# Step inputs of a selective scan replicated by DMA through DRAM instead of by TensorE, and step sizes three pairs deep

## The chip, the cores and the metric

One core of one Trainium2 chip runs the whole program. The metric is the device time of one execution in microseconds, lower is better. The times of a kernel are given as the median of several executions; the profile is one further execution, with its own time.

## The reference, cut to what matters

The program is a chain of four convolution-like layers on an array `x` of shape (16, 32, 128, 128). The change lies in layer 1, in its state-space ("mamba") part. Two directions over a sequence of length 16384, with 18 inner channels and 16 states:

```python
def selective_scan(u, dt, A, Bm, Cm, D):
    dA = jnp.exp(dt[..., None] * A)
    dBu = dt[..., None] * Bm[:, :, None, :] * u[..., None]
    def comb(e1, e2):
        a1, b1 = e1
        a2, b2 = e2
        return (a2 * a1, a2 * b1 + b2)
    _, h = jax.lax.associative_scan(comb, (dA, dBu), axis=1)
    return jnp.einsum('bldn,bln->bld', h, Cm) + u * D

def run(xz_, A_log_):
    xi, z = jnp.split(xz_, 2, axis=-1)
    xi = jax.nn.silu(causal_dwconv1d(xi.transpose(0, 2, 1), conv1d_w, conv1d_b)).transpose(0, 2, 1)
    x_dbl = xi @ x_proj_w.T
    dt = jax.nn.softplus(x_dbl[..., :DT_RANK] @ dt_proj_w.T + dt_proj_b)
    Bm = x_dbl[..., DT_RANK:DT_RANK + D_STATE]
    Cm = x_dbl[..., DT_RANK + D_STATE:]
    y = selective_scan(xi, dt, -jnp.exp(A_log_), Bm, Cm, D_ssm)
    return y * jax.nn.silu(z)
```

So each (batch, channel) row of `dt` and of `dt * u` is needed 16 times, once for each state: for the decay `exp(dt * A)` and for the product with `Bm`.

## The kernel before, in words

The stage is the function `state_space` (from L738). Its work is cut into 128 chunks (`N = 4 * NC`: two directions, two halves of the batch, 32 pieces of 512 positions), which follow one another. A chunk holds 8 batch rows. A tile for the scan has 128 partitions (8 batch rows times 16 states) and 512 columns, and belongs to one of the 18 channels. Two channels make a pair, so a chunk is 9 pairs, p = 0 to 8; channels 0 to 9 are half 0 and channels 10 to 17 are half 1. Each engine runs its own list of instructions in order, and semaphores tie the lists together. The tail of each engine's list for chunk i already holds the projections of chunk i+1.

One pair goes through the engines like this:

- GpSimd (`steps`, L1174) makes the step sizes `dts[:, un, hf, 0]` = softplus and the step inputs `dts[:, un, hf, 1]` = step size times `xi`, 128x512 each, half 0 of the next chunk after its outputs of pair 5 and half 1 after those of pair 7.
- TensorE replicates a channel's 8 rows over the 16 states with a 0/1 matrix `sl`: `rates_of` (L891) into the PSUM tile `pr` (2 banks, one pair deep), and `inputs_of` (L897) into the PSUM tile `pu` (4 banks, two pairs deep). `replicate` (L916) issues the inputs of pair p+1 and the rates of pair p+2. Before both it waits until the scan has left the bank (`wait_inputs`) and until the exponential has read `pr` (`wait_rates`).
- ScalarE (`decays`, L1060) turns `pr` into the decays `da` in SBUF, two pairs ahead; between them it does the gates, the softplus and the copies of the projections of the next chunk, which all go through one PSUM bank `pp` in a fixed order (L1083 to L1109).
- VectorE (`inputs_by_b`, L1131) multiplies `pu` in place with `bs` (L1138, two instructions a pair), and (`scans`, L1140) runs the recurrence (L1148, two a pair): `da` from SBUF, `pu` from PSUM, result `hs` in SBUF, three pairs deep. Twice a chunk `skip` (L1151) adds the direct term to the reduced outputs.
- GpSimd (`outputs`, L1187) carries the last column on (L1193) and multiplies `hs` with `cs` (L1196), both 18 times a chunk, and multiplies with the gate (`gated`, L1180) twice. The scan of pair p+3 waits until the outputs of pair p are done.
- TensorE reduces over the states (`reduce`, L930) and projects out (`out_proj`, L885); ScalarE copies the result to `osb` (L1058), once a chunk and 129 times in all.
- SyncE loads the sequences (L821, six DMAs a chunk) and the rates (L824, L825) of chunk i+2, and stores chunk i-1 (L829).

Of the kernel before, what the change touches and what calls it, by code (L numbers as in the profile page):

```python
# [8 lines left out]
P = 128  # L9
# [728 lines left out]
def state_space(nc, seq, w_x, w_z, conv_rows, conv_b, w_dt, dt_rows, dt_b, w_b, w_c, a_log, keeps, d_skip, w_out,  # L738
# [4 lines left out]
    N = 4 * NC  # L743
    KEEP = D_IN
    USES = 9
    X0, Z0, X1, Z1, DT0, DT1, BB, CC, OUT = range(USES)
    LAST_OF = {0: 1, 1: 1, 2: 3, 3: 3, 4: 4, 5: 6, 6: 6, 7: 8, 8: 8}

    with ExitStack() as ctx:
# [59 lines left out]
        @block.sync  # L809
        def _(sp):  # L810
            weights = ((wx, w_x), (wz, w_z), (crow, conv_rows), (wdt, w_dt), (drow, dt_rows), (wb, w_b), (wc, w_c), (wo, w_out), (sl, sel), (slt, sel_t))
            for dst, src in weights:
                sp.dma_start(dst[:], src).then_inc(w_load, 16)
            for n, src in enumerate((conv_b, dt_b, d_skip)):
                sp.dma_start(cols[:, n, :], src).then_inc(w_load, 16)

            def load(i, u):
                taps = (0, 1, 1, 2, 2, 3)
                rows = seq[at(i)].rearrange("i p n -> (i p) n")
                for tap, (tile, to, first, n) in zip(taps, TAP_PARTS):  # L820
                    sp.dma_start(sq[to:to + n, u, tile, :], rows[first:first + n, tap:tap + LC]).then_inc(s_in[u], 16)  # L821

            def load_rates(i, u):
                sp.dma_start(al[:, u, 0:D_IN], a_log[at(i)].rearrange("i p n -> (i p) n")).then_inc(a_in[u], 16)  # L824
                sp.dma_start(al[:, u, KEEP:], keeps[at(i), :].broadcast_to([NB, 1])).then_inc(a_in[u], 16)  # L825

            def store(i, u, use):
                sp.wait_ge(pp_drained, use + 1)
                sp.dma_start(mixed[at(i)].rearrange("i p n -> (i p) n"), osb[:, u, :]).then_inc(stored[u], 16)  # L829

            for n in range(2):
                load(n, n)
                load_rates(n, n)

            def chunk(i, j, u, last):

                sp.wait_ge(pp_drained, use_of(i, Z1) + 1)
                load(i + 2, u)
                sp.wait_ge(carry_ready, i * D_IN + D_IN)
                load_rates(i + 2, u)  # L840
                store(i, u, use_of(i + 1, OUT))

            with sp.Fori(0, N // 2 - 1) as j:
                for u in range(2):
                    chunk(j * 2 + u, j, u, False)
            store(N - 2, 0, use_of(N - 1, OUT))
            store(N - 1, 1, use_of(N, 0))
            store(N, 0, use_of(N, 1))
            sp.wait_ge(stored[0], 16 * (N // 2 + 2))
            sp.wait_ge(stored[1], 16 * (N // 2 + 1))  # L850

        @block.tensor
        def _(pe):
# [37 lines left out]
            def rates_of(i, u, p, part):  # L891
                hf, q, run = place(2 * p + part)
                rows = slice(32 * q, 32 * q + 32)
                pe.matmul(pr[:, LC * part:LC * (part + 1)], sl[rows, run, :], dts[rows, u, hf, 0, :],  # L894
                          start=True, stop=True, tile_position=(32 * q, 0)).then_inc(rates_done, 1)

            def inputs_of(i, u, p, part):  # L897
                hf, q, run = place(2 * p + part)
                rows = slice(32 * q, 32 * q + 32)
                bank = 2 * ((u + p) % 2) + part  # L900
                pe.matmul(pu[:, LC * bank:LC * (bank + 1)], sl[rows, run, :], dts[rows, u, hf, 1, :],  # L901
                          start=True, stop=True, tile_position=(32 * q, 0)).then_inc(inputs_done, 1)

            def wait_inputs(i, p):

                if p in (0, HALF_PAIRS):
                    pe.wait_ge(dtu_ready, i * 2 + (1 + p // HALF_PAIRS))
                pe.wait_ge(scan_done, i * D_IN + (2 * p + 4))

            def wait_rates(i, p):  # L910

                if p in (0, HALF_PAIRS):
                    pe.wait_ge(dt_ready, i * 2 + (1 + p // HALF_PAIRS))
                pe.wait_ge(exp_done, i * D_IN + (2 * p + 2))

            def replicate(i, u, p, last):  # L916

                ahead = [(i, u, p + k) if p + k < PAIRS else (i + 1, 1 - u, p + k - PAIRS) for k in (1, 2)]
                if not (last and p + 1 >= PAIRS):
                    wait_inputs(ahead[0][0], ahead[0][2])  # L920
                if not (last and p + 2 >= PAIRS):
                    wait_rates(ahead[1][0], ahead[1][2])
                for part in range(2):
                    if not (last and p + 1 >= PAIRS):
                        inputs_of(*ahead[0], part)
                for part in range(2):
                    if not (last and p + 2 >= PAIRS):
                        rates_of(*ahead[1], part)
# [33 lines left out]
            wait_inputs(0, 0)
            wait_rates(0, 0)
            for part in range(2):
                inputs_of(0, 0, 0, part)
            for part in range(2):
                rates_of(0, 0, 0, part)
            wait_rates(0, 1)
            for part in range(2):
                rates_of(0, 0, 1, part)  # L970
# [40 lines left out]
        def _(act):  # L1011
# [103 lines left out]
        def _(dve):  # L1115
# [15 lines left out]
            def inputs_by_b(i, u, p):  # L1131
# [1773 lines left out]
```

## Time and profile before

| | |
|---|---|
| median of 3 executions | 20994.22 us (20714.11, 21013.87, 20994.22) |
| profiled execution | 20821.64 us, of which its span is 20820.1 us |
| state-space stage in the profile | starts near 7180 us, ends near 12760 us |
| busy share of the span | PE 79%, DVE 67%, ACT 62%, POOL 46% |
| mean granted TensorE clock | 0.855 of 2.4 GHz |

PE is TensorE, DVE VectorE, ACT ScalarE, POOL GpSimd, SP SyncE. A tile is named with the prefix of its stage: `l1m` is the state-space stage, `l1y` the one after it, `l1d` the one after that, `l3a` a late one. "Idle before" an instruction is time in which its engine did nothing, with what ended it behind the arrow.

### The profile page before, as it was taken

How to read it: one execution, taken by the hardware profiler on the slowest of the kernel's cores; microseconds unless marked ns; L12 is line 12 of the kernel's file. 1: busy time of each engine (PE TensorE's matmuls, PEld its weight loads, DVE VectorE, ACT ScalarE, POOL GpSimd, SP SyncE). 2: the span in 40 equal slices, each digit the busy share in tenths (PEclk: the TensorE clock that was granted, in tenths of full speed). 3: DMA queues.
4: the chain of work that ended last, by engine and by line, in shares of the span. 5: the costliest groups of instructions: out<-in, count | busy, mean ns of one | idle time of the engine just before them, and what ended most of it. 6: DMA issues, size and time to landing. Idle time of an engine off the chain costs nothing. (4 is left out here: it accounts for less than half of the span.)

```text
span 20820.1 us, 421401 instructions
## 1 busy us (share of the span) xinstructions
PE 16358.0 (79%) x158640; PEld 6982.2 (34%) x158640; DVE 14027.1 (67%) x13848; ACT 12953.3 (62%) x21322; POOL 9553.7 (46%) x7800
## 2 busy tenths in 40 slices
PE   6888888888845388888888887699989996336997
PEld 2333333333311022222222222355454453004664
DVE  8999999999951377777777775465565566123322
ACT  6899999988943277777777774466666665220101
POOL 5787877877720177777777775011111111000002
PEclk9999999999977688888888888677787788667988
DMA  2000000000049400000000003221112112993333
GB/s 74 12 11 12 11 12 11 12 12 11 12 114 163 113 17 17 17 17 17 17 17 17 17 17 74 32 31 28 31 31 31 29 31 77 186 209 81 79 68 124
DMA packets 1433366, 986.00 MB, mean 47 GB/s; under 512 B 783816, under 2 KB 1296944, under 8 KB 1399864
## 3 DMA queue, kind: packets, MB, share of 16 engines
q1 hardware_dynamic: 1335848, 837.05, 19.7%
q0 software_dynamic: 17408, 67.11, 1.2%
q10 hardware_dynamic: 79056, 66.70, 1.0%
q8 instruction: 793, 12.99, 0.3%
q14 instruction: 261, 2.14, 0.0%
HBM read 759.05 MB, written 211.63 MB: 47 GB/s over the span
## 5 line engine op out<-in xcount | busy, mean ns | idle before, releaser
L270 DVE TENSOR_TENSOR l_mx<-l_p_v,l_puN 128x2048 f32<-128x2048 f32 x2560 | 5635.7, 2281 | 142.4 <-PE l_p_s L485 129.6
L485 PE MATMUL l_p_s<-l_mx,l_w2z 128*32 128x512 f32 x32768 | 3818.9, 610 | 582.5 <-ACT l_mx L397 313.0
L290 POOL TENSOR_TENSOR l_mx<-l_pv,l_puP 128x2048 f32<-128x2048 f32 x1024 | 3715.6, 3645 | 317.9 <-PE l_p_s L485 312.1
L1196 POOL TENSOR_TENSOR l1m_hc<-l1m_hs,l1m_cs 128x512 f32<-128x512 f32 x2304 | 2922.8, 1269 | 8.5 <-DVE l1m_hs L1148 8.1
L1148 DVE TENSOR_TENSOR_SCAN l1m_hs<-l1m_da,l1m_carry,l1m_pu 128x512 f32<-128x512 f32 x2304 | 2824.1, 1268 | 106.1 <-ACT l1m_da L1066 2.2
L1790 ACT ACTIVATE l1d_ab<-l1d_pt 128x1024 f32<-128x1024 f32 x2304 | 2311.9, 1024 | 611.5 <-DVE l1d_hat L1668 305.6
L416 ACT ACTIVATE l_mx<-l_pv,l_puP 128x128 f32<-128x128 f32 x8192 | 2446.8, 393 | 0.8
L1668 DVE TENSOR_SCALAR l1d_hat<-l1d_ab 128x1024 f32<-128x1024 f32 x2304 | 1923.2, 836 | 443.8 <-ACT l1d_ab L1790 321.0
L1138 DVE TENSOR_TENSOR l1m_pu<-l1m_pu,l1m_bs 128x512 f32<-128x512 f32 x2304 | 1477.1, 687 | 1100.9 <-PE l1m_pu L901 1100.9
L1587 PE MATMUL l1d_po<-l1d_hat,l1d_ring 128*32 128x128 f32 x36864 | 1799.7, 322 | 358.7 <-DVE l1d_hat L1668 233.2
L485 PEld LDWEIGHTS l_p_s<-l_mx,l_w2z 128*32 128x32 f32 x32768 | 982.3, 112 | 3017.5 <-issue 1764.6
L397 ACT ACTIVATE l_mx<-l_mx 128x2048 f32<-128x2048 f32 x1024 | 1954.4, 1909 | 50.8 <-POOL l_mx L290 50.4
L1841 POOL TENSOR_TENSOR l1d_res<-l1d_res,l1d_so 128x2048 f32<-128x2048 f32 x32 | 119.4, 3731 | 3951.8 <-DVE l1d_to L1727 3949.5
L1066 ACT ACTIVATE l1m_da<-l1m_pr,l1m_an 128x512 f32<-128x512 f32 x2304 | 1458.9, 684 | 565.3 <-PE l1m_pr L894 399.9
L901 PE MATMUL l1m_pu<-l1m_dts,l1m_sl 32*128 32x512 f32 x4608 | 1416.0, 691 | 480.4 <-ACT l1m_da L1066 470.7
L1569 PE MATMUL l1d_pg<-l1d_wz,l1d_im 32*128 32x288 f32 x5120 | 1472.5, 656 | 22.1 <-DMA l1d_im<-x_after 10.1
L1655 DVE COPY l1d_ring<-l1d_pg 128x288 f32<-128x288 f32 x1280 | 585.7, 458 | 1323.5 <-PE l1d_pg L1569 1321.8
L1587 PEld LDWEIGHTS l1d_po<-l1d_hat,l1d_ring 128*32 128x32 f32 x36864 | 1030.3, 124 | 1262.9 <-issue 807.2
L894 PE MATMUL l1m_pr<-l1m_dts,l1m_sl 32*128 32x512 f32 x4608 | 1403.2, 687 | 2.7 <-ACT l1m_da L1066 2.7
L2064 POOL TENSOR_TENSOR l3a_lm<-l3a_lmask,l3a_ln 128x1320 f32<-128x1320 f32 x16 | 47.8, 2990 | 2381.2 <-ACT l3a_ln L2015 2381.2
L1776 ACT ACTIVATE l1d_ring<-l1d_pg 128x288 f32<-128x288 f32 x1280 | 526.3, 411 | 877.5 <-PE l1d_pg L1569 876.8
L1552 PE MATMUL l1d_pt<-l1d_yt,l1d_rw 32*128 32x512 bf16 x4608 | 1047.5, 450 | 18.8 <-issue 17.2
(330 smaller groups left out, 22896.5 us busy)
## 6 DMA issues: line engine op xcount, KB each, us to landing
n_xt<-x_after SPq DMA_DIRECT2D x48, 2048.0 KB
l1o_img<-x_after SPq DMA_DIRECT2D x32, 2032.0 KB, 17.2
l_img<-x_after SPq DMA_DIRECT2D x32, 2032.0 KB, 16.9
l1m_sq<-seq SPq DMA_DIRECT2D x256, 144.0 KB
n_xt<-in_x_dram SPq DMA_DIRECT2D x16, 2048.0 KB
l_xs<-in_x_dram SPq DMA_DIRECT2D x128, 256.0 KB, 2.9
x_after<-l_ot SPq DMA_DIRECT2D x128, 256.0 KB, 2.4
l1o_img<-x_after SPq DMA_DIRECT2D x16, 2048.0 KB, 16.9
```

The source lines that it names most:

```text
L270: v.tensor_tensor(mx[:, r % QB, :, :, :], columns.unsqueeze(1).broadcast_to([P, 4, G, P]), rows.broadcast_to([P, 4, G, P]), ALU.max).then_ ...
L290: g.tensor_tensor(mx[:, r % QB, :, :, :], pv[:, u, :, :].unsqueeze(1).broadcast_to([P, 4, G, P]), rows.broadcast_to([P, 4, G, P]), ALU.add ...
L397: act.activation(tile, tile, ACT.Relu).then_inc(max_by_g, 1)
L416: ins = act.activation(mx[:, r % QB, q, t, :], pv[:, u, t, :], ACT.Relu, bias=puP[:, u, t, R * q + r:R * q + r + 1])
L485: ins = pe.matmul(p_s[R * q:R * (q + 1), 512 * u:512 * (u + 1)], w2z[:, 31 - r:63 - r], mx[:, r % QB, q, :, :].rearrange("p t v -> p (t v) ...
L1138: dve.tensor_tensor(tile, tile, bs[:, u, :], ALU.mult).then_inc(dbu_done, 1)
L1148: dve.tensor_tensor_scan(hs[:, p % 3, part, :], da[:, p % 3, part, :], pu[:, LC * bank:LC * (bank + 1)], carry[:, u, c:c + 1], ALU.mult, A ...
L1196: g.tensor_tensor(hc[:, (3 * u + p) % 6, part, :], hs[:, p % 3, part, :], cs[:, u, :], ALU.mult).then_inc(hc_done, 1)
L1569: pe.matmul(pg[:, 512 * half_strip:512 * half_strip + KO], im[C * g:C * (g + 1), :, col_at(g, j)], wz[C * g:C * (g + 1), u, :], start=True ...
L1587: ins = pe.matmul(po[C * g:C * (g + 1), 512 * (s % 2):512 * (s % 2) + P], ring[:, (8 * u + s + k) % RING, g, k, :], hat[:, m % 3, n % 2, P ...
L1668: v.tensor_scalar(hat[:, m % 3], ab[:, m % 2], 1.0, 1.0, ALU.min, ALU.subtract).then_inc(hat_done, 1)
L1790: act.activation(ab[:, m % 2].rearrange("p a n -> p (a n)"), pt[:, 1024 * (m % 2):1024 * (m % 2 + 1)], ACT.Abs).then_inc(abs_done, 1)
```

## The change

- The step inputs are no longer replicated by TensorE. SyncE writes a half of them (128x512, 256 KB) to a DRAM tensor `steps_u`, waits until the write has landed (`write_steps`), and then reads each channel's 8 rows back with 16 copies of each row, into one of six SBUF slots of `rp` (`replicas`, two DMAs of 256 KB a pair).
- The product with `bs` is one VectorE instruction over a pair, 128x1024, in place in `rp`, and the scan reads `rp`. Both tensor inputs of the product, and both of the scan, now lie in SBUF.
- `pu` is gone; `pr` has 6 banks, three pairs deep. `replicate` issues the rates of pair p+3 alone and waits only for the exponential of pair p and for new step sizes.
- SyncE's list is written out for all 128 chunks. In it, the replicas of pair p+6 follow the scan of pair p; the write of half 0 of the next chunk stands at p = 3 and that of half 1 at p = 8; the load of the sequences stands at p = 2, the loads of the rates and the store at the chunk's end.

```diff
+    SLOTS = 6
+    steps_u = nc.dram_tensor("step_inputs", [2, 2, P, LC], F32).ap()
...
+        rp = m.sb("rp", [NB, SLOTS, 2, LC])
...
-        pr = m.bank("pr", 2)
-        pu = m.bank("pu", 4)
+        pr = m.bank("pr", 6)
...
+            def write_steps(n, un, hf):
+                sp.wait_ge(dtu_ready, n * 2 + (hf + 1))
+                sp.dma_start(steps_u[un, hf], dts[:, un, hf, 1, :]).then_inc(steps_out, 16)
+                sp.wait_ge(steps_out, n * 32 + (16 * hf + 16))
+            def replicas(un, p):
+                slot = (3 * un + p) % SLOTS
+                for part in range(2):
+                    hf, q, run = place(2 * p + part)
+                    first = 32 * q + HB * run
+                    sp.dma_start(rp[:, slot, part, :], steps_u[un, hf, first:first + HB].unsqueeze(1).broadcast_to([HB, D_STATE, LC])
+                                 ).then_inc(rep_in[slot], 16)
...
+            def chunk(i, u, more, last):
+                for p in range(PAIRS):
+                    q = p + SLOTS
+                    if q < PAIRS or not last:
+                        sp.wait_ge(scan_done, i * D_IN + (2 * p + 8))
+                    if q < PAIRS:
+                        replicas(u, q)
+                    elif not last:
+                        if q - PAIRS in (0, HALF_PAIRS):
+                            write_steps(i + 1, 1 - u, (q - PAIRS) // HALF_PAIRS)
+                        replicas(1 - u, q - PAIRS)
+                    if p == 2 and more:
+                        sp.wait_ge(pp_drained, use_of(i, Z1) + 1)
+                        load(i + 2, u)
+                if more:
+                    sp.wait_ge(carry_ready, i * D_IN + D_IN)
+                    load_rates(i + 2, u)
+                store(i, u, use_of(N, 0) if last else use_of(i + 1, OUT))
...
             def replicate(i, u, p, last):
...
+                n, un, q = (i, u, p + 3) if p + 3 < PAIRS else (i + 1, 1 - u, p + 3 - PAIRS)
+                if not (last and p + 3 >= PAIRS):
+                    if q in (0, HALF_PAIRS):
+                        pe.wait_ge(dt_ready, n * 2 + (1 + q // HALF_PAIRS))
+                    pe.wait_ge(exp_done, i * D_IN + (2 * p + 4))
+                    for part in range(2):
+                        rates_of(n, un, q, part)
...
-                dve.wait_ge(inputs_done, i * D_IN + (2 * p + 2))
-                for part in range(2):
-                    bank = 2 * ((u + p) % 2) + part
-                    tile = pu[:, LC * bank:LC * (bank + 1)]
-                    dve.tensor_tensor(tile, tile, bs[:, u, :], ALU.mult).then_inc(dbu_done, 1)
+                slot, uses = (3 * u + p) % SLOTS, (PAIRS * u + p) // SLOTS
+                dve.wait_ge(rep_in[slot], j * (32 * 3) + 32 * (uses + 1))
+                tile = rp[:, slot]
+                dve.tensor_tensor(tile, tile, bs[:, u, :].unsqueeze(1).broadcast_to([NB, 2, LC]), ALU.mult).then_inc(dbu_done, 2)
...
-                    dve.tensor_tensor_scan(hs[:, p % 3, part, :], da[:, p % 3, part, :], pu[:, LC * bank:LC * (bank + 1)],
+                    dve.tensor_tensor_scan(hs[:, p % 3, part, :], da[:, p % 3, part, :], rp[:, (3 * u + p) % SLOTS, part, :],
                                            carry[:, u, c:c + 1], ALU.mult, ALU.add).then_inc(scan_done, 1)
```

## Rows read from the trace of the kernel before

**Rows 1.** All instructions of L1058, the last copy of each chunk: min/median/max, first and last start.

```profile
L1058 ACT ACTIVATE l1m_osb<-l1m_pp x129: 593/593/595, 7235.6 to 12759.1; 72x512 f32<-72x512 f32 x129
```

**Rows 2.** Busy time by engine in 500 us of the stage (clock, DMA share, GB/s last).

```profile
10000.00:10500.00 500.00, 434.40 (x1670) 132.49 (x1668) 395.21 (x439) 351.90 (x471) 371.58 (x483) 0.87 0.06 16
```

**Rows 3.** The page's groups by line: busy us, mean ns | idle before, releaser.

```profile
L1138 DVE TENSOR_TENSOR l1m_pu<-l1m_pu,l1m_bs 128x512 f32<-128x512 f32 x2304 | 1477.1, 687 | 1100.9 <-PE l1m_pu L901 1100.9
...
L901 PE MATMUL l1m_pu<-l1m_dts,l1m_sl 32*128 32x512 f32 x4608 | 1416.0, 691 | 480.4 <-ACT l1m_da L1066 470.7
```

**Rows 4.** VectorE in order of time in one chunk: start us, us, instructions, idle before.

```profile
10041.67 1.30 DVE L1138 TENSOR_TENSOR l1m_pu<-l1m_pu,l1m_bs 128x512 f32<-128x512 f32 x2 [6.03 <-PE l1m_pu L901]
...
10056.75 1.30 DVE L1138 TENSOR_TENSOR l1m_pu<-l1m_pu,l1m_bs 128x512 f32<-128x512 f32 x2 [2.51 <-PE l1m_pu L901]
...
10060.50 1.27 DVE L1138 TENSOR_TENSOR l1m_pu<-l1m_pu,l1m_bs 128x512 f32<-128x512 f32 x2
10061.87 2.45 DVE L1148 TENSOR_TENSOR_SCAN l1m_hs<-l1m_da,l1m_carry,l1m_pu 128x512 f32<-128x512 f32 x2
```

**Rows 5.** ScalarE's waits in the 500 us of rows 2: us in total, times, longest.

```profile
ACT l1m_da L1066 <- PE l1m_pr L894: 35.0, 43, 1.4
...
ACT l1m_da L1066 <- DVE l1m_hs L1148: 15.3, 12, 1.3
```

**Rows 6.** Products from SBUF alone, before the stage's chunks start: durations ns min/median/max.

```profile
L1126 DVE TENSOR_TENSOR l1m_wtap<-l1m_wx,l1m_crow x1: 949/949/949, 7143.4 to 7143.4; 96x768 f32<-96x768 f32 x1
...
L1128 DVE TENSOR_TENSOR l1m_wdtm<-l1m_wdt,l1m_drow x2: 411/412/414, 7144.2 to 7144.6; 128x256 f32<-128x256 f32 x2
```

**Rows 7.** VectorE lines with one tensor input in PSUM: durations ns min/median/max.

```profile
L1138 DVE TENSOR_TENSOR l1m_pu<-l1m_pu,l1m_bs x2304: 671/690/700, 7181.8 to 12746.5; 128x512 f32<-128x512 f32 x192
...
L1148 DVE TENSOR_TENSOR_SCAN l1m_hs<-l1m_da,l1m_carry,l1m_pu x2304: 1252/1268/1282, 7185.3 to 12748.5; 128x512 f32<-128x512 f32 x192
...
L1352 DVE TENSOR_TENSOR l1y_v<-l1y_acc,l1y_base x16: 2277/2286/2287, 12801.3 to 13045.2; 72x2048 f32<-72x2048 f32 x16
```

**Rows 8.** VectorE lines with all operands in SBUF: durations ns min/median/max.

```profile
L1668 DVE TENSOR_SCALAR l1d_hat<-l1d_ab x2304: 668/685/5830, 13216.1 to 17561.4; 128x1024 f32<-128x1024 f32 x192
...
L1361 DVE TENSOR_SCALAR l1y_y<-l1y_v x16: 1223/1224/4973, 12804.9 to 13058.0; 72x2048 f32<-72x2048 f32 x16
...
L2118 DVE TENSOR_SCALAR l3a_lns<-l3a_ln,l3a_st x16: 3129/3194/3249, 18840.3 to 20024.9; 128x264 f32<-128x264 f32 x16
```

**Rows 9.** VectorE and GpSimd in order of time, two places of the later stages.

```profile
12836.55 1.22 DVE L1356 TENSOR_SCALAR l1y_v<-l1y_v 72x2048 f32<-72x2048 f32 x1
12837.81 4.97 DVE L1361 TENSOR_SCALAR l1y_y<-l1y_v 72x2048 f32<-72x2048 f32 x1
...
12836.94 4.76 POOL L1280 TENSOR_TENSOR l1y_r<-l1y_y,l1y_piece 72x2048 f32<-72x2048 f32 x1 [3.82 <-ACT l1y_piece L1302]
12843.78 4.07 POOL L1285 TENSOR_TENSOR l1y_r<-l1y_r,l1y_piece 72x2048 f32<-72x2048 f32 x1 [2.08 <-issue]
...
13547.95 4.80 DVE L1668 TENSOR_SCALAR l1d_hat<-l1d_ab 128x1024 f32<-128x1024 f32 x1
...
13547.35 4.86 POOL L1850 TENSOR_TENSOR l1d_res<-l1d_res,l1d_xr 128x2048 f32<-128x2048 f32 x1
```

**Rows 10.** GpSimd's groups in the 500 us of rows 2: busy us, mean ns | idle before.

```profile
L1196 POOL TENSOR_TENSOR l1m_hc<-l1m_hs,l1m_cs 128x512 f32<-128x512 f32 x206 | 261.4, 1269 | 0.0
L1193 POOL TENSOR_TENSOR l1m_carry<-l1m_hs,l1m_al 128x1 f32<-128x1 f32 x207 | 39.2, 189 | 113.7 <-DVE l1m_hs L1148 112.3
L1178 POOL TENSOR_TENSOR l1m_dts<-l1m_dts,l1m_xi 128x512 f32<-128x512 f32 x24 | 30.4, 1267 | 1.9
```

**Rows 11.** SyncE's issues: six in order of time; then two DMA groups, KB each, us to landing.

```profile
10066.94 2.81 SPq L821 DMA_DIRECT2D l1m_sq<-seq  x6
...
l_xs<-in_x_dram SPq DMA_DIRECT2D x128, 256.0 KB, 2.9
x_after<-l_ot SPq DMA_DIRECT2D x128, 256.0 KB, 2.4
```

More of the change, by code:

```diff
@@ L784, in state_space @@
         py = m.bank("py")
-        pr = m.bank("pr", 2)
-        pu = m.bank("pu", 4)
+        pr = m.bank("pr", 6)
         (w_load, w_ready, a_exp, a_ready, pp_full, pp_drained, ab, e3, lg_ready, dt_ready, dtu_ready,
-         rates_done, inputs_done, exp_done, dbu_done, scan_done, carry_ready, hc_done, y_done, y1_done, y2_done) = (m.sem(n) for n in (
+         rates_done, exp_done, dbu_done, scan_done, carry_ready, hc_done, y_done, y1_done, y2_done) = (m.sem(n) for n in (
              "w_load w_ready a_exp a_ready pp_full pp_drained ab e3 lg_ready dt_ready dtu_ready "
-             "rates_done inputs_done exp_done dbu_done scan_done carry_ready hc_done y_done y1_done y2_done").split())
+             "rates_done exp_done dbu_done scan_done carry_ready hc_done y_done y1_done y2_done").split())
         s_in = [m.sem("s_in0"), m.sem("s_in1")]
         a_in = [m.sem("a_in0"), m.sem("a_in1")]
+        steps_out = m.sem("steps_out")
+        rep_in = [m.sem(f"rep_in{n}") for n in range(SLOTS)]
         stored = [m.sem("stored0"), m.sem("stored1")]
@@ L833, in _ @@
                 load_rates(n, n)
[L835 to L847, printed above, removed]
+            for hf in range(2):
+                write_steps(0, 0, hf)
+            for p in range(SLOTS):
+                replicas(0, p)
+            def chunk(i, u, more, last):
[16 more added lines that the diff above has]
+                store(i, u, use_of(N, 0) if last else use_of(i + 1, OUT))
+            for i in range(N):
+                chunk(i, i % 2, i < N - 2, i == N - 1)
             store(N, 0, use_of(N, 1))
@@ L893, in rates_of @@
                 rows = slice(32 * q, 32 * q + 32)
-                pe.matmul(pr[:, LC * part:LC * (part + 1)], sl[rows, run, :], dts[rows, u, hf, 0, :],
+                bank = 2 * (p % 3) + part
+                pe.matmul(pr[:, LC * bank:LC * (bank + 1)], sl[rows, run, :], dts[rows, u, hf, 0, :],
                           start=True, stop=True, tile_position=(32 * q, 0)).then_inc(rates_done, 1)
-            def inputs_of(i, u, p, part):
-                hf, q, run = place(2 * p + part)
-                rows = slice(32 * q, 32 * q + 32)
-                bank = 2 * ((u + p) % 2) + part
[L901 to L914, printed above, removed]
-            def replicate(i, u, p, last):
[L918 to L922, printed above, removed]
-                for part in range(2):
[L924 to L928, printed above, removed]
+            def replicate(i, u, p, last):
+                n, un, q = (i, u, p + 3) if p + 3 < PAIRS else (i + 1, 1 - u, p + 3 - PAIRS)
[5 more added lines that the diff above has]
+                        rates_of(n, un, q, part)
             def reduce(i, u, pairs):
@@ L961, in _ @@
             c_proj(0, 0, 2)
[L962 to L970, printed above, removed]
+            pe.wait_ge(dt_ready, 1)
+            for p in range(3):
+                for part in range(2):
+                    rates_of(0, 0, p, part)
             def chunk(i, j, u, last):
@@ L1065, in decays @@
                 for part in range(2):
-                    act.activation(da[:, p % 3, part, :], pr[:, LC * part:LC * (part + 1)], ACT.Exp,
+                    act.activation(da[:, p % 3, part, :], pr[:, LC * (2 * (p % 3) + part):LC * (2 * (p % 3) + part + 1)], ACT.Exp,
                                    scale=an[:, u, 2 * p + part:2 * p + part + 1]).then_inc(exp_done, 1)
@@ L1129, in _, with inputs_by_b @@
             ins.then_inc(w_ready, 1)
-            def inputs_by_b(i, u, p):
+            def inputs_by_b(i, j, u, p):
                 if p == 0:
                     dve.wait_ge(pp_drained, use_of(i, BB) + 1)
-                dve.wait_ge(inputs_done, i * D_IN + (2 * p + 2))
-                for part in range(2):
-                    bank = 2 * ((u + p) % 2) + part
-                    tile = pu[:, LC * bank:LC * (bank + 1)]
-                    dve.tensor_tensor(tile, tile, bs[:, u, :], ALU.mult).then_inc(dbu_done, 1)
+                slot, uses = (3 * u + p) % SLOTS, (PAIRS * u + p) // SLOTS
+                dve.wait_ge(rep_in[slot], j * (32 * 3) + 32 * (uses + 1))
+                tile = rp[:, slot]
+                dve.tensor_tensor(tile, tile, bs[:, u, :].unsqueeze(1).broadcast_to([NB, 2, LC]), ALU.mult).then_inc(dbu_done, 2)
             def scans(i, u, p):
@@ L1145, in scans @@
                 for part in range(2):
-                    bank = 2 * ((u + p) % 2) + part
                     c = 2 * p + part
-                    dve.tensor_tensor_scan(hs[:, p % 3, part, :], da[:, p % 3, part, :], pu[:, LC * bank:LC * (bank + 1)],
+                    dve.tensor_tensor_scan(hs[:, p % 3, part, :], da[:, p % 3, part, :], rp[:, (3 * u + p) % SLOTS, part, :],
                                            carry[:, u, c:c + 1], ALU.mult, ALU.add).then_inc(scan_done, 1)
@@ L1159, in chunk @@
                 for p in range(PAIRS):
-                    inputs_by_b(i, u, p)
+                    inputs_by_b(i, j, u, p)
                     scans(i, u, p)
```

## The prediction

> **What bounds the kernel now.** I read the stage first: the last copy of a chunk (L1058) runs 129 times [rows 1], so a chunk takes (12759.1 - 7235.6) / 128 = 43.15 us, and every microsecond a chunk is worth 128 us. The busy times of 500 us inside the stage [rows 2], times 43.15 / 500, give each engine's work a chunk: PE 37.5, DVE 34.1, ACT 30.4, POOL 32.1 us. None is full. Then the groups by line: DVE waits 1100.9 us in the stage for the replicated inputs in `pu`, 8.6 us a chunk [rows 3]. 34.1 + 8.6 = 42.7 of 43.15: DVE's work and this one wait make the chunk. DVE in order of time shows where: 6.03 us at one pair, 2.51 at another, and in between a pair is 1.27 us of products and 2.45 us of scans with nothing before them [rows 4]. TensorE's list is in order, and the inputs of the next pair stand behind projections that wait for ScalarE; that is why they come late.
>
> **Parts that take work away.** The inputs leave TensorE: 1416.0 us, 11.1 us a chunk [rows 3]. TensorE at 26.4 us then bounds nothing, even if its granted clock fell from 0.87 to the lower of its two levels, 0.5 or 1.2 GHz (26.4 x 0.87 / 0.5 = 46 us, under the chunk that I forecast). DVE's wait for `pu` goes. The product becomes one instruction of 1024 columns with both inputs in SBUF: 768 columns take 949 ns and 256 take 412 [rows 6], 1.05 ns a column, so 1.22 us in place of 1.27 [rows 4], 0.5 us a chunk less. The scan keeps its 2.45 us a pair, since its pace (1268 ns for 512 columns [rows 7], against 690 for a product) is that of the recurrence. DVE's work becomes 33.6 us.
>
> **DMAs and waits that it adds, at nothing.** SyncE issues 20 more DMAs a chunk. Six in a row take 2.81 us [rows 11], 0.47 each, so 9.4 us of a queue that is else nearly empty. Their traffic: 16 GB/s over 500 us is 8.0 MB, and a share of 0.06 of 16 engines is 480 engine-us [rows 2], 60 us a MB, so 15.7 engine-us for 256 KB. 20 of them are 315, or 19.7 us a chunk on all 16 engines and 39.3 if half of the engines take part. Both fit under the chunk that I forecast.
> How many engines a DMA uses no row shows. The Trainium skill ("DMA: Bandwidth & Descriptors", section on why a DMA increments its semaphore by 16) says that it is the largest number up to 16 that divides the slowest dimension on both sides; here these are 8 and 128, so 8 engines and the 39.3.
> SyncE waits in `write_steps` for the next chunk's step inputs. Queued behind it are replicas of the next chunk alone, the rates and the store, none due before the chunk's end; the replicas of pairs 6 to 8 stand ahead. Half 0 is made after GpSimd's pair 5. GpSimd can lag by three pairs (`hs`), so at worst the scans are then at pair 8, and one pair is left for two POOL instructions (2.5 us), a write and a read (2.4 and 2.9 us [rows 11]) and issues. That can be some 3 us late. While DVE waits for it, GpSimd works off its arrears, which DVE would meet later; I take nothing, and 6 us a chunk (the write, the read and the issues in full) as the upper end. TensorE's wait for new step sizes moves one pair ahead (p = 6 and p = 2); behind it stand `c_proj` and a reduction, due at the next chunk's first outputs. I take nothing; uncovered it costs no more than the scans of the pair by which it moved, 2.45 us, and the 6 us cover that.
>
> **What decides: two SBUF inputs beside GpSimd.** So far each product and scan read one tensor from PSUM. Such lines never vary beside GpSimd: 671 to 700, 1252 to 1282, 2277 to 2287 ns [rows 7]. Lines whose operands all lie in SBUF do: 668 to 5830 ns, 1223 to 4973, and 264 columns that always take 3.1 us or more [rows 8]. Order of time shows why [rows 9]. DVE's L1361 starts 0.87 us after POOL's 4.76 us instruction and ends at 12842.78, 1.08 us after it: it did its 1.22 us of work when POOL was done. L1668 the same, 0.54 us after a POOL instruction of 4.86. And POOL's L1280, begun under DVE's L1356, takes 4.76 where L1285 of the same shape takes 4.07: it waited until L1356 ended. The two exclude each other for a whole instruction, and about 0.14 us (1.22 - 1.08) is saved at each handover.
> After the change every product and scan has both tensor inputs in SBUF, and GpSimd works 32.1 us a chunk on SBUF. Rows 8 are single-input lines at two columns a ns or nearly; a two-input line at one column a ns beside GpSimd no row shows. The bounds: no exclusion (as rows 7, which have the operations), or full exclusion (as rows 8, which have the place of the operands). I take full exclusion: what parts the varying lines from the steady ones in this trace is where the operands lie; L1352 is a two-input product of 2048 columns and is steady with one of them in PSUM.
> The Trainium skill ("SBUF — State Buffer", section "Who interferes with whom") says that a VectorE instruction with two SBUF inputs contends with a GpSimd instruction that reads SBUF, the second to start being blocked until the first is done. That is the case which no row shows; by it the sum is the one below, without it that of the first rival.
>
> **The sum.** A chunk is then DVE's work and POOL's end to end.
> - Lower end, each instruction less 0.14: DVE 9 x (1.08 + 2 x 1.13) = 30.1; POOL 24 of 128x512 (18 outputs, 2 gates, 4 steps, all like 1267 ns [rows 10]) x 1.13 = 27.1; 18 carries of 0.19 [rows 10] less 0.14 = 0.9. Together 58.1 us.
> - Upper end, nothing saved: 9 x (1.22 + 2.45) = 33.0, and POOL's 32.1: 65.1 us.
> `skip`, with one input in PSUM, lies beside POOL. I take the middle, 61.6 us, 18.45 more than now: x 128 = 2362 us on the profiled execution's 20821.6, so 23180 us. The median shown lies 0.8% above the profiled execution; I leave that to the range.
>
> **The rivals.**
> 1. No exclusion at this pace (ends on the other side). DVE needs 33.6 us and ScalarE's chain is next: 30.4 us of work, and of its idle 148.1 us in rows 2 the waits for the rates (35.0) and for the scan (15.3) [rows 5] go, which leaves 97.8, 8.4 us a chunk. 38.8 us a chunk: 4.35 x 128 = 557 less, 20265 us, 2.7% faster; 33.6 us would be 19600. For it: the products and scans of rows 7 never varied. Against: they had PSUM inputs. It decides if the scan's mean stays at 1.27 us beside POOL.
> 2. Only the product excludes, the scan does not (it takes a column every 2.5 ns). Each of 9 products waits for one POOL instruction, 1.13: DVE 33.6 + 10.2 = 43.8 us, 0.65 x 128 = 83 more, 20905 us.
> 3. The replicas bound: on 4 engines, or at twice the time a packet on 8, 78.6 us a chunk, 35.4 x 128 = 4530 more, 25350 us. For it: 16 copies of one row come from one place in DRAM. Against: the stage moves 16 GB/s now [rows 2], so there is room, and the slots are six pairs deep.
>
> **How the numbers follow.** 0.80 for the forecast: all of rows 8 vary and none of rows 7, but none has this pace with two inputs. 0.12 for the first rival, 0.05 for the second, 0.03 for the third. The forecast's own ends are 58.1 us (20821.6 + 14.95 x 128 = 22735) and 65.1 + 6 = 71.1 us (24400); 1.5% below for the spread of the runs shown gives 22400 to 24400, which holds the 0.80. A measurement of this kernel tells about 2% from no change. Slower by over 2%: the forecast and the third rival, 0.83. Within 2%: the second, and a quarter of the first, 0.08. Faster: the rest of the first, 0.09.
>
> **What would show it.** Right: the scan's durations spread far above 1.27 us, GpSimd's outputs above 1.27 us, and DVE and POOL are each stretched so that their busy times overlap on paper although a chunk is near 61 us; ScalarE waits for the scan (`da` free) where it waited for rates; DVE hardly waits for a DMA into `rp`. Wrong: scans and outputs steady at 1.27 us, a chunk under 43 us (first rival); only the product stretched (second); DVE idle before the product until a DMA lands, in every pair (third). If it is in the first pair of a chunk alone, the late write of half 0 was under-priced.

## The result and the profile after

The kernel after takes 23104.89 us (median of 4, 23035.26 to 23158.41), the one before beside it 20955.86 us: 1.1048 times as long, with a 95% interval of 1.0968 to 1.1128 (the quotient of the two medians is 1.1026). The forecast was 23180 us. The profiled execution of after took 23076.47 us, with a span of 23074.9 and a mean granted clock of 0.799.

The last copy of a chunk again gives the chunk's time, as [rows 1] did (durations min/median/max, first and last start):

```profile
L1062 ACT ACTIVATE l1m_osb<-l1m_pp x129: 593/593/598, 7255.0 to 14816.2; 72x512 f32<-72x512 f32 x129
```

(14816.2 - 7255.0) / 128 = 59.07 us a chunk for 43.15, so 2038 of the 2255 us by which the span grew lie in the stage. Nearly all the rest, 199 us, lies in the stage `l1d`, whose code is unchanged: 4544.8 us from its first to its last matmul for 4346.0, at a granted clock of 0.73 where the profile of before has 0.79 (each the mean of a stretch with both levels in it). Its most frequent matmul, before and then after:

```profile
L1587 PE MATMUL l1d_po<-l1d_hat,l1d_ring x36864: 269/273/423, 13216.9 to 17562.6; 128*32 128x128 f32 x200
L1589 PE MATMUL l1d_po<-l1d_hat,l1d_ring x36864: 269/297/423, 15276.2 to 19820.7; 128*32 128x128 f32 x200
```

The same 500 us as in [rows 2], then the page's groups by line, for [rows 3, 7, 10]:

```profile
10000.00:10500.00 500.00, 366.24 (x887) 104.11 (x884) 430.63 (x243) 251.51 (x339) 442.59 (x350) 0.72 0.30 102
```

```profile
L1150 DVE TENSOR_TENSOR_SCAN l1m_hs<-l1m_da,l1m_carry,l1m_rp 128x512 f32<-128x512 f32 x2304 | 4822.5, 2132 | 698.2 <-POOL l1m_carry L1195 575.1
...
L1198 POOL TENSOR_TENSOR l1m_hc<-l1m_hs,l1m_cs 128x512 f32<-128x512 f32 x2304 | 3467.7, 1505 | 3.5 <-DVE l1m_hs L1150 3.5
...
L1195 POOL TENSOR_TENSOR l1m_carry<-l1m_hs,l1m_al 128x1 f32<-128x1 f32 x2286 | 2007.4, 878 | 733.1 <-DMA l1m_al<-in_keeps_dram 721.1
...
L1141 DVE TENSOR_TENSOR l1m_rp<-l1m_rp,l1m_bs 128x1024 f32<-128x1024 f32 x1152 | 1730.3, 1502 | 273.2 <-DMA l1m_rp<-step_inputs 273.2
```

DVE and POOL look nearly full, 86% and 89% of the window, although their work hardly changed. The mean durations say why: a scan takes 2132 ns where it took 1268, an output 1505 for 1269, and a carry, which works on one column, 878 for 189. That is time spent waiting inside an instruction, and it counts as busy. Two true waits are new: POOL's 721.1 us for a DMA into `al`, the rates, 5.6 us a chunk, and DVE's 575.1 us for POOL's carry behind it. The wait for the replicas is 273.2 us. Its longest, 44.3 us, is at the start of the stage; the rest is 1.8 us a chunk, and falls on the chunk's first pair.

VectorE and GpSimd in order of time, within one chunk (start us, us, idle before in brackets):

```profile
10083.18 4.53 DVE L1150 TENSOR_TENSOR_SCAN l1m_hs<-l1m_da,l1m_carry,l1m_rp 128x512 f32<-128x512 f32 x2 [1.33 <-POOL l1m_carry L1195]
10087.63 1.19 DVE L1141 TENSOR_TENSOR l1m_rp<-l1m_rp,l1m_bs 128x1024 f32<-128x1024 f32 x1
10088.91 4.43 DVE L1150 TENSOR_TENSOR_SCAN l1m_hs<-l1m_da,l1m_carry,l1m_rp 128x512 f32<-128x512 f32 x2
```

```profile
10083.08 1.26 POOL L1198 TENSOR_TENSOR l1m_hc<-l1m_hs,l1m_cs 128x512 f32<-128x512 f32 x1
10084.30 1.10 POOL L1195 TENSOR_TENSOR l1m_carry<-l1m_hs,l1m_al 128x1 f32<-128x1 f32 x1
10085.36 1.27 POOL L1198 TENSOR_TENSOR l1m_hc<-l1m_hs,l1m_cs 128x512 f32<-128x512 f32 x1
10086.59 1.10 POOL L1195 TENSOR_TENSOR l1m_carry<-l1m_hs,l1m_al 128x1 f32<-128x1 f32 x1
10087.65 2.33 POOL L1198 TENSOR_TENSOR l1m_hc<-l1m_hs,l1m_cs 128x512 f32<-128x512 f32 x1
```

The first scan of the pair waits for the output that ends at 10084.34. The carry that POOL issues next waits for the scan, and so takes 1.10 us. Then comes an output, under which the second scan waits, and so on: one scan and one output every 2.29 us. The output at 10087.65 begins with the product at 10087.63, and ends 1.16 us after it.

SyncE in order of time, then its waits for the writes in the window (us in total, times, longest):

```profile
10039.78 0.34 SPq L838 DMA_DIRECT2D step_inputs<-l1m_dts  x1
10041.78 6.34 SPq L847 DMA_DIRECT2D l1m_rp<-step_inputs  x10
10052.41 0.34 SPq L838 DMA_DIRECT2D step_inputs<-l1m_dts  x1
10060.68 1.21 SPq L847 DMA_DIRECT2D l1m_rp<-step_inputs  x2
10061.93 0.46 SPq L828 DMA_DIRECT2D l1m_al<-in_a_log_dram  x1
10062.43 0.43 SPq L829 DMA_DIRECT2D l1m_al<-in_keeps_dram  x1
```

```profile
SPq L847 <- DMA step_inputs<-l1m_dts: 64.4, 16, 9.0
```

The write of half 0 is followed 2.0 us later by the first replica that needs it. The write of half 1 is issued behind ten replicas of 256 KB on the same queue, and its successor comes only 8.3 us later; until then the DMA engines stay half busy (a share of 0.48 to 0.69 from 10048 to 10060 us, 0.02 in the two us after). Over the stage this second write takes 3.3 to 10.2 us, with a median of 5.9. The rates stand behind that; `al` lands when GpSimd has waited 7.70 us for it.

### The profile page after: what moved, and what is told of

It is laid out like the page before. It is cut to its first block and busy times, and to the rows that moved or that the text cites. A ratio compares the mean times of both kernels' runs of the same rounds, so it can differ in the third digit from the quotient of the medians.

```text
span 23074.9 us, 411139 instructions
## 1 busy us (share of the span) xinstructions
PE 17335.3 (75%) x154032; PEld 7173.7 (31%) x154032; DVE 16273.5 (71%) x12696; ACT 12919.8 (56%) x21322; POOL 12288.8 (53%) x7800
## 3 DMA queue, kind: packets, MB, share of 16 engines
q14 instruction: 291, 2.38, 0.0%
## 5 line engine op out<-in xcount | busy, mean ns | idle before, releaser
L1150 DVE TENSOR_TENSOR_SCAN l1m_hs<-l1m_da,l1m_carry,l1m_rp 128x512 f32<-128x512 f32 x2304 | 4822.5, 2132 | 698.2 <-POOL l1m_carry L1195 575.1
L1198 POOL TENSOR_TENSOR l1m_hc<-l1m_hs,l1m_cs 128x512 f32<-128x512 f32 x2304 | 3467.7, 1505 | 3.5 <-DVE l1m_hs L1150 3.5
L1195 POOL TENSOR_TENSOR l1m_carry<-l1m_hs,l1m_al 128x1 f32<-128x1 f32 x2286 | 2007.4, 878 | 733.1 <-DMA l1m_al<-in_keeps_dram 721.1
L1589 PE MATMUL l1d_po<-l1d_hat,l1d_ring 128*32 128x128 f32 x36864 | 1900.9, 337 | 334.1 <-DVE l1d_hat L1670 216.0
L926 PE MATMUL l1m_pr<-l1m_dts,l1m_sl 32*128 32x512 f32 x4608 | 1688.1, 818 | 430.5 <-POOL l1m_dts L1178 425.0
L1141 DVE TENSOR_TENSOR l1m_rp<-l1m_rp,l1m_bs 128x1024 f32<-128x1024 f32 x1152 | 1730.3, 1502 | 273.2 <-DMA l1m_rp<-step_inputs 273.2
L1571 PE MATMUL l1d_pg<-l1d_wz,l1d_im 32*128 32x288 f32 x5120 | 1539.0, 685 | 21.1 <-DMA l1d_im<-x_after 9.7
L1589 PEld LDWEIGHTS l1d_po<-l1d_hat,l1d_ring 128*32 128x32 f32 x36864 | 1080.2, 129 | 1317.1 <-issue 876.8
L901 PE MATMUL l1m_pp<-l1m_xi,l1m_wdtm 128*128 128x512 f32 x1024 | 800.1, 926 | 689.2 <-ACT l1m_sz L1034 673.9
L1554 PE MATMUL l1d_pt<-l1d_yt,l1d_rw 32*128 32x512 bf16 x4608 | 1101.8, 473 | 24.1 <-issue 22.6
```

What stands on the lines that cost most here:

```text
L1141: dve.tensor_tensor(tile, tile, bs[:, u, :].unsqueeze(1).broadcast_to([NB, 2, LC]), ALU.mult).then_inc(dbu_done, 2)
L1195: g.tensor_tensor(carry[:, 1 - u, c:c + 1], hs[:, p % 3, part, LC - 1:], al[:, 1 - u, KEEP:], ALU.mult).then_inc(carry_ready, 1)
L1198: g.tensor_tensor(hc[:, (3 * u + p) % 6, part, :], hs[:, p % 3, part, :], cs[:, u, :], ALU.mult).then_inc(hc_done, 1)
L1589: ins = pe.matmul(po[C * g:C * (g + 1), 512 * (s % 2):512 * (s % 2) + P], ring[:, (8 * u + s + k) % RING, g, k, :], hat[:, m % 3, n % 2, P ...
```

## The experiments

The theory is that of the forecast: a VectorE instruction with two SBUF inputs and a GpSimd instruction exclude each other, so that the one that starts second waits until the first is done. Its rivals are the new DMAs and waits, and an effect of the product alone. "Before" beside the first four was 20941.94 us (median of 7), beside the last three 20935.15 (median of 17). Ratios are to it, with 95% intervals; they differ by up to 0.3% from the quotients of the medians shown. The time of a chunk is read from one profiled execution of each kernel.

**The scan alone, in the kernel before.** No DMA of the change; the product goes to SBUF (VectorE reads one input from PSUM there) and the scan reads two inputs from SBUF.

```diff
+        di = m.sb("di", [NB, 4, LC])
-                    dve.tensor_tensor(tile, tile, bs[:, u, :], ALU.mult).then_inc(dbu_done, 1)
+                    dve.tensor_tensor(di[:, bank, :], tile, bs[:, u, :], ALU.mult).then_inc(dbu_done, 1)
-                    dve.tensor_tensor_scan(hs[:, p % 3, part, :], da[:, p % 3, part, :], pu[:, LC * bank:LC * (bank + 1)],
+                    dve.tensor_tensor_scan(hs[:, p % 3, part, :], da[:, p % 3, part, :], di[:, bank, :],
```

> The kernel before, with one edit: the product is written to an SBUF tile, and the scan reads that in place of PSUM. So the scan has two SBUF inputs, the product one; there is no DMA path and no new order. Exclusion whenever both tensor inputs of a VectorE instruction lie in SBUF: the scan's mean rises from 1.27 to about 2 us, GpSimd's outputs and carries rise too, and a chunk is at least the 18 scans less the handover (18 x 1.13 = 20.3 us) and GpSimd's 28 to 32 us, 48 to 53 us in place of 43.15, so 21450 to 22100 us. Rival, the time of the changed kernel comes from its DMA path and its new waits: scan steady at 1.27 us, chunk within 1 us of 43.15, time unchanged. Rival, only the product excludes: the same as the second.

Measured: 21654.7 us (4 executions), 1.0348 [1.0292, 1.0403]; 49.13 us a chunk. Groups of 500 us of this kernel:

```profile
L1149 DVE TENSOR_TENSOR_SCAN l1m_hs<-l1m_da,l1m_carry,l1m_di 128x512 f32<-128x512 f32 x184 | 367.6, 2036 | 8.3
L1139 DVE TENSOR_TENSOR l1m_di<-l1m_pu,l1m_bs 128x512 f32<-128x512 f32 x182 | 115.0, 670 | 6.5 <-PE l1m_pu L902 6.4
...
L1197 POOL TENSOR_TENSOR l1m_hc<-l1m_hs,l1m_cs 128x512 f32<-128x512 f32 x182 | 230.3, 1265 | 0.0
L1194 POOL TENSOR_TENSOR l1m_carry<-l1m_hs,l1m_al 128x1 f32<-128x1 f32 x182 | 125.9, 692 | 35.3 <-DVE l1m_hs L1149 35.3
```

Moving one operand of the scan from PSUM to SBUF stretches it to 2036 ns, while the product with one PSUM input stays at 670. GpSimd's carries rise to 692 ns as expected; its outputs, expected to rise too, stay at 1265: here it is the scan and the carry that do the waiting. The exclusion does not need the change's DMAs, and it holds for a scan, at one column every 2.5 ns, which the second rival denied.

**The product alone, in the kernel after.** The product writes to PSUM and the scan reads from there. The product's own inputs both stay in SBUF. `pr` gives up a pair of its banks for it.

```diff
+        pu = m.bank("pu", 2)
-                dve.tensor_tensor(tile, tile, bs[:, u, :].unsqueeze(1).broadcast_to([NB, 2, LC]), ALU.mult).then_inc(dbu_done, 2)
+                dve.wait_ge(scan_done, i * D_IN + (2 * p + 6))
+                dve.tensor_tensor(pu[:].rearrange("p (b n) -> p b n", b=2), tile, bs[:, u, :].unsqueeze(1).broadcast_to([NB, 2, LC]), ALU.mult).then_inc(dbu_done, 2)
```

> The changed kernel, with the product written to two PSUM banks and the scan reading it there, so that only the product has two SBUF inputs; the rates are two pairs deep in four banks. Exclusion by operands: the scan is steady at 1.27 us, the product's mean lies between 1.2 and 2.4 us, and a chunk is VectorE's 33.6 us and at most 9 waits of 1.13, so 40 to 46 us, 20400 to 21200 us. Rival, the DMA path and the waits: these are all still there, so near the changed kernel's 59 us a chunk. Rival, only the product excludes: also near 59.

Measured: 22107.75 us (4), 1.0588 [1.0521, 1.0655]; 51.43 us a chunk, far above what was expected. The page's groups of this kernel:

```profile
L1152 DVE TENSOR_TENSOR_SCAN l1m_hs<-l1m_da,l1m_carry,l1m_pu 128x512 f32<-128x512 f32 x2304 | 2823.5, 1267 | 1202.3 <-POOL l1m_carry L1197 849.7
L1143 DVE TENSOR_TENSOR l1m_pu<-l1m_rp,l1m_bs 128x1024 f32<-128x1024 f32 x1152 | 1905.7, 1654 | 302.7 <-DMA l1m_rp<-step_inputs 193.1
...
L1197 POOL TENSOR_TENSOR l1m_carry<-l1m_hs,l1m_al 128x1 f32<-128x1 f32 x2286 | 844.6, 369 | 1477.2 <-DMA l1m_al<-in_keeps_dram 1463.4
```

The scan is steady at 1267 ns and the product is stretched (mean 1654), as forecast, but POOL now waits 1463.4 us for `al`, 11.4 us a chunk. The late rates, seen as a symptom in the kernel after, look like a cost of their own, which the next three experiments test.

**No VectorE instruction with two SBUF inputs.** As the last one, with `bs` in PSUM too; everything else of the change stays (`pr` one pair deep makes room).

```diff
-        bs = m.sb("bs", [NB, 2, LC])
-        pr = m.bank("pr", 6)
+        pr = m.bank("pr", 2)
+        pu = m.bank("pu", 2)
+        bs = m.bank("bs", 2)
-                dve.tensor_tensor(tile, tile, bs[:, u, :].unsqueeze(1).broadcast_to([NB, 2, LC]), ALU.mult).then_inc(dbu_done, 2)
+                dve.tensor_tensor(pu[:].rearrange("p (b n) -> p b n", b=2), tile, bs[:, LC * u:LC * (u + 1)].unsqueeze(1).broadcast_to([NB, 2, LC]), ALU.mult).then_inc(dbu_done, 2)
```

> The changed kernel, with the copy of B in two PSUM banks and the product written to two PSUM banks, so that product and scan each have one SBUF input; the rates go back to one pair deep, two pairs ahead. The replicas by DMA, the write through DRAM and SyncE's order are as in the changed kernel. Exclusion: product near 1.2 us and scan at 1.27 us, both steady, GpSimd's outputs steady at 1.27 us, and a chunk is ScalarE's chain, 38.8 to 43 us, so 20250 to 20900 us. Rival, the DMA path and the new waits are the cost: near 59 us a chunk, 23000 us.

Measured: 21866.92 us (4), 1.0445 [1.0376, 1.0514]; 50.05 us a chunk. Groups of the same 500 us:

```profile
L1153 DVE TENSOR_TENSOR_SCAN l1m_hs<-l1m_da,l1m_carry,l1m_pu 128x512 f32<-128x512 f32 x180 | 220.6, 1267 | 109.4 <-POOL l1m_carry L1198 79.2 <-ACT l1m_da L1072 25.2 <-POOL l1m_hc L1201 1.0
L1144 DVE TENSOR_TENSOR l1m_pu<-l1m_rp,l1m_bs 128x1024 f32<-128x1024 f32 x90 | 110.5, 1228 | 20.6 <-DMA l1m_rp<-step_inputs 14.0
...
L1201 POOL TENSOR_TENSOR l1m_hc<-l1m_hs,l1m_cs 128x512 f32<-128x512 f32 x180 | 228.3, 1269 | 0.0
L1198 POOL TENSOR_TENSOR l1m_carry<-l1m_hs,l1m_al 128x1 f32<-128x1 f32 x179 | 34.2, 191 | 125.5 <-DMA l1m_al<-in_keeps_dram 125.5
```

Every duration is back at its free value, carry included. The exclusion is gone, and 9.0 us a chunk went with it. The expected 43 us or less was not reached, because POOL now waits 125.5 us in 500 for the rates, and DVE 79.2 us for POOL.

**The rates earlier.** The kernel after with the loads of the rates at p = 2, ahead of both writes.

```diff
-                if more:
-                    sp.wait_ge(carry_ready, i * D_IN + D_IN)
-                    load_rates(i + 2, u)
+                        sp.wait_ge(carry_ready, i * D_IN + D_IN)
+                        load_rates(i + 2, u)
```

> The changed kernel, with the loads of the rates moved from the chunk's end to p = 2, ahead of the writes of the step inputs that SyncE waits for. GpSimd's 721 us of waits for that load go. If VectorE and GpSimd together are the bound, VectorE used that time for its own instructions, and a chunk stays between 58 and 59 us: 0 to 150 us less. Rival, the wait is on the path: 5.6 us a chunk, some 720 us less, 22400 us.

Measured: 22816.02 us (4), 1.0916 [1.0848, 1.0983]; 57.02 us a chunk. Groups of 500 us:

```profile
L1149 DVE TENSOR_TENSOR_SCAN l1m_hs<-l1m_da,l1m_carry,l1m_rp 128x512 f32<-128x512 f32 x158 | 350.8, 2258 | 6.6
...
L1197 POOL TENSOR_TENSOR l1m_hc<-l1m_hs,l1m_cs 128x512 f32<-128x512 f32 x157 | 228.0, 1452 | 0.0
L1194 POOL TENSOR_TENSOR l1m_carry<-l1m_hs,l1m_al 128x1 f32<-128x1 f32 x158 | 174.8, 1106 | 0.0
```

POOL waits for nothing any more and yet the chunk is only 2.05 us shorter, more than the 1 us expected at most and far less than the rival's 5.6: while POOL stood and waited in the kernel after, DVE ran free (at 10061.26 a pair of scans took 2.46 us there, for the 4.53 shown), so the wait of 5.6 us was in good part used. This is the exclusion nearly by itself: a chunk is DVE's and POOL's work end to end, 57.02 us where the sum's lower end was 58.1.

**Both undone together.** The edits of the last two experiments in one kernel.

```diff
-        pr = m.bank("pr", 6)
+        pr = m.bank("pr", 2)
+        pu = m.bank("pu", 2)
+        bs = m.bank("bs", 2)
...
+                        sp.wait_ge(carry_ready, i * D_IN + D_IN)
+                        load_rates(i + 2, u)
```

> The kernel of the earlier run in which product and scan have one PSUM input each, and besides the loads of the rates at p = 2, as in the run that moved them alone. In that earlier run the exclusion was gone and a chunk still took 50.05 us, with GpSimd waiting 13.9 us a chunk for the rates. Two costs, exclusion and late rates, each hiding the other: a chunk falls to ScalarE's chain, 38.8 to 43 us, 20250 to 20950 us, and the replicas and the write through DRAM cost next to nothing. Rival, a third cost sits in the DMA path (8 engines for a replica, 39 us a chunk by the estimate): VectorE waits for the replicas in every pair, and a chunk stays at 45 to 50 us.

Measured: 20771.47 us (10), 0.9942 [0.9906, 0.9978]; 41.09 us a chunk, within what was expected. Its window, and VectorE's groups in it:

```profile
10000.00:10500.00 500.00, 434.35 (x1311) 129.25 (x1309) 418.62 (x354) 374.36 (x503) 393.26 (x513) 0.90 0.42 147
```

```profile
L1152 DVE TENSOR_TENSOR_SCAN l1m_hs<-l1m_da,l1m_carry,l1m_pu 128x512 f32<-128x512 f32 x220 | 269.6, 1267 | 40.1 <-ACT l1m_da L1071 32.5 <-DVE l1m_pu L1143 1.2
L1143 DVE TENSOR_TENSOR l1m_pu<-l1m_rp,l1m_bs 128x1024 f32<-128x1024 f32 x110 | 135.1, 1228 | 23.0 <-DMA l1m_rp<-step_inputs 14.9 <-DVE l1m_hs L1152 0.2
L1159 DVE SCALAR_TENSOR_TENSOR l1m_y<-l1m_xi,l1m_cols,l1m_py 128x512 f32<-128x512 f32 x24 | 17.6, 735 | 17.8 <-PE l1m_py L948 17.8
```

The two causes account for the loss: 41.09 + 9.0 for the late rates (50.05), or + 15.9 for the exclusion (57.02), and together 59.07, since each hides part of the other (`pr` is one pair deep in the first two of these, three pairs in the others). The replicas are not a third: their traffic is higher here (a DMA share of 0.42 and 147 GB/s) at 41.09 us a chunk, and the wait for them is 14.9 us in 500. What the change would have brought without the two causes is 2.06 us a chunk, or 0.6% of the whole time, against the 10% that it cost. DVE's 8.6 us for `pu` gave way to waits for the decays (32.5 us in 500), the reduced outputs (17.8) and the replicas (14.9).

**Outputs that only write.** The kernel after with early rates, and GpSimd's 18 outputs made by a memset: the product with C is left out, and so is its reading of SBUF. The carry keeps reading; the wait for a free output slot now stands ahead of it.

```diff
-                g.tensor_tensor(hc[:, (3 * u + p) % 6, part, :], hs[:, p % 3, part, :], cs[:, u, :], ALU.mult).then_inc(hc_done, 1)
+                g.memset(hc[:, (3 * u + p) % 6, part, :], 0.5).then_inc(hc_done, 1)
```

> The changed kernel with the rates loaded at p = 2, and GpSimd's 18 outputs a chunk made by writing a constant to SBUF, without reading; this leaves out the product with C. Product and scan keep their two SBUF inputs. GpSimd's carries, gates and steps still read. If VectorE waits only for GpSimd instructions that read SBUF: the scan's mean falls from 2.26 us to under 1.7, the writes overlap the scans, and a chunk is 39 to 46 us. Rival, any GpSimd instruction on SBUF excludes: each of 18 writes still takes its turn, the scan's mean stays at 1.9 us or more, and a chunk is 9 x 3.3 us of VectorE and GpSimd's turns end to end, 48 us or more.

Measured: 20929.91 us (one execution), 43.31 us a chunk. The scan's group in 500 us, then VectorE and GpSimd in order of time:

```profile
L1149 DVE TENSOR_TENSOR_SCAN l1m_hs<-l1m_da,l1m_carry,l1m_rp 128x512 f32<-128x512 f32 x204 | 272.7, 1377 | 23.3 <-ACT l1m_da L1069 15.8
```

```profile
10061.51 2.24 DVE L1140 TENSOR_TENSOR l1m_rp<-l1m_rp,l1m_bs 128x1024 f32<-128x1024 f32 x1 [3.68 <-DMA l1m_rp<-step_inputs]
...
10066.17 1.20 DVE L1140 TENSOR_TENSOR l1m_rp<-l1m_rp,l1m_bs 128x1024 f32<-128x1024 f32 x1
```

```profile
10061.40 1.27 POOL L1183 TENSOR_TENSOR l1m_y<-l1m_y,l1m_sz 128x512 f32<-128x512 f32 x1
...
10066.17 0.52 POOL L1197 MEMSET l1m_hc<- 128x512 f32 x1
10066.65 0.76 POOL L1196 TENSOR_TENSOR l1m_carry<-l1m_hs,l1m_al 128x1 f32<-128x1 f32 x1
```

The scan's mean falls from 2258 to 1377 ns, as expected if only reads exclude. Beside a memset begun at the same time, the product takes its 1.20 us and the memset 0.52, so that it has ended 0.68 us before the product; beside the gate, which reads, it takes 2.24. The carry behind the memset, which reads one column, waits for the product's end. So it is GpSimd's reading that excludes, however little it reads. The memset is also shorter than an output, so the chunk's time alone would not separate the two; the durations do.

**The order on TensorE, in the kernel before.** The change's aim, inputs that come in time, without leaving PSUM: the inputs of pair p+1 are issued before the wait for the rates' bank, and the projection for the gate one pair later.

```diff
-                if not (last and p + 2 >= PAIRS):
-                    wait_rates(ahead[1][0], ahead[1][2])
                 for part in range(2):
...
                         inputs_of(*ahead[0], part)
+                if not (last and p + 2 >= PAIRS):
+                    wait_rates(ahead[1][0], ahead[1][2])
...
-                        z_proj(n, un, 1)
...
                         if p == 3:
+                            z_proj(n, un, 1)
                             dt_proj(n, un, 0)
```

> The kernel before with TensorE's list reordered and nothing else: the inputs of pair p+1 are issued before the wait for the rates' bank, and the second z projection of the next chunk goes behind the replication at p = 3. If VectorE's 8.6 us a chunk for the replicated inputs came from TensorE's order: most of that wait goes, and a chunk is 39 to 41.5 us, 20250 to 20650 us, faster than both kernels. Rival, the wait only moves to the decays, since ScalarE's chain is as late as TensorE's inputs: the scan waits for ScalarE and a chunk stays within 1 us of 43.15.

Measured: 20664.54 us (6), 0.9889 [0.9843, 0.9934]; 40.77 us a chunk. DVE's wait in the kernel before, then DVE's group in this one, each in the same 500 us, show the part of the wait that is left:

```profile
DVE l1m_pu L1138 <- PE l1m_pu L901: 95.5, 32, 6.0
...
L1138 DVE TENSOR_TENSOR l1m_pu<-l1m_pu,l1m_bs 128x512 f32<-128x512 f32 x220 | 141.4, 689 | 67.9 <-PE l1m_pu L901 67.9
```

67.9 us in 500 is 5.5 us a chunk, for 8.2 in the same window of before: a third of the wait has gone, not most of it as expected. The granted clock in this window also rose, from 0.87 to 0.94, and no run tells how much of the gain is the clock's. The chunk lies in the range expected, the time 15 us above its range. This version has the lowest median of the study, though its interval overlaps with that of "Both undone together", and it changes only the order.

## Why the prediction was right, and where its steps were off

- **What bounds the kernel before: borne out in part.** Issuing the inputs earlier shortened the chunk by 2.38 us, 2.7 of the wait having gone, with a higher granted clock. The other 5.5 us of the wait were not removed.
- **Full exclusion: shown from both sides.** It appears with one operand moved to SBUF, and goes when the operands return to PSUM. The rule of the Trainium skill ("SBUF — State Buffer", section "Who interferes with whom") says that two SBUF inputs contend with a GpSimd instruction that reads SBUF and not with one that only writes; the products of 2.24 and 1.20 us above agree with both halves. One reading behind the forecast was loose: the lines of [rows 8] run at 1.5 to 1.7 columns a ns at their fastest, not at two; the argument does not hang on it.
- **The sum: its middle was too high.** The step "I take the middle, 61.6 us" mis-sized the saving at each handover, taking half. It is had nearly every time: one scan, one carry and one output take 2.29 us in the rows above, where the lower end has 1.13 + 0.05 + 1.13. Exclusion with the rates in time is 57.02 us, even 1.1 us below the lower end of 58.1; where that last 1.1 us comes from was not traced.
- **"The rates and the store, none due before the chunk's end": wrong.** The rates that SyncE loads at the end of a chunk are read by GpSimd's first carry of the next, and SyncE waits up to 9.0 us for a write in front of them. The write was priced at 2.4 us from an idle queue [rows 11]; behind ten replicas it takes 5.9 (median). Only the write of half 0 was looked at; half 1, behind the ten replicas, was not. The cost is 2.05 us a chunk beside the exclusion and 9.0 without it.
- **The write of half 0: late, as foreseen.** "Some 3 us late" measured 1.8 us ((273.2 - 44.3) / 127), in the first pair. It was taken as nothing because DVE and POOL share the chunk, and with early rates the two add up to it with 7.5 us of this wait in 500 left. What it costs without exclusion no run separates.
- **DMA: right.** (0.30 x 16 x 500) / (102 x 0.5 MB) is 47 engine-us a MB, for the 60 estimated. While only replicas and the write behind them move (10054 to 10058 us), the DMA share is 0.53, about the half of the engines that the forecast reckoned with. The replicas keep DVE waiting in one pair of nine, so the third rival falls.
- **One sign did not come.** ScalarE was to wait for the scan, where it had waited for rates. In the 500 us it waits 0.5 us for the scan; its longest waits are 80.3 us for GpSimd's product with the gate and 52.4 us for the projection of C.
- **The first rival's price** was off too: without exclusion it had 38.8 us, and the runs show 50.05, or 41.09 with early rates (`pr` one pair deep, which that sum did not have).
- **The second rival** falls, since it denied that a scan is excluded, and the first experiment shows one that is (2036 ns). What the products alone cost was not measured: they are stretched in the second experiment, but the late rates cover its chunk, and no run has it with early rates.
- **The total is nearer than its terms.** In the stage 2362 us were forecast and 2038 came; 199 us came in `l1d`, of which nothing was forecast. That stage takes 4346.0 to 4590.5 us in the eight other profiles of this study, all with the same code there, and the profile of before is the shortest of them; why its clock differs stays open. So the mechanism was right, while part of the closeness of 23180 us to the profile's 23076.47 is luck: 324 us too much in the stage against 217 us elsewhere that were not forecast.

## What to carry to other kernels

Before moving a VectorE operand from PSUM to SBUF, count the instructions that then have both inputs in SBUF and what GpSimd reads at the time: the two add up instead of overlapping, and the profile shows it as busy time on both. A one-column instruction of 0.9 us is the plainest sign. Where an in-order DMA queue waits for a write, list what stands behind it, and price the write by what is queued ahead of it, not by an idle queue.

## What was not expected of the hardware

- GpSimd's read of a single column waits for a whole scan or product (carry 189 ns free, 1106 with early rates), and the output behind it then goes ahead of DVE's next instruction, so that the engines take turns by scan and by carry with output.
- A 256 KB write that lands in some 2 us on an idle queue took 3.3 to 10.2 (median 5.9) behind ten replicas of 256 KB on the same queue, where it is issued a median of 4.3 us after the last of them: 7.7 us in one chunk where it came 2.45 us behind, 3.3 in one where it came 6.3 behind. In "Both undone together", where it comes 0.1 us behind, the median is 10.0.
- The removal of a true wait of 5.6 us a chunk (POOL's for the rates) returned 2.05, because the other engine had run free meanwhile.
